# A gated cross-attention with a mixture of experts: shorter routing, another root, a folded bias

## What is computed

```python
x = x + tanh(g_xattn) * xattn(layernorm(x), ctx)    # 8 x 128 channels x 256, 16 heads of 8 channels
x = x + tanh(g_ffn) * ffn(layernorm(x))             # 1024 tokens of 256, 32 experts + a shared one

# xattn:  q = Wq x + bq; k = Wk c + bk; v = Wv c + bv; p = softmax(q k / sqrt(8)); Wo (p v) + bo
# ffn, routing of a token:
scores = sigmoid(x @ w_router)                      # 32 experts
sfc = scores + corr_bias
group_scores = top_k(sfc.reshape(T, 8, 4), 2).sum(-1)   # the two best of each group of four
keep the 4 best groups; among their experts the 6 best by sfc
routed = sum over the 6 of scores[e] * expert_e(x)
shared = silu(x @ sh_gate) * (x @ sh_up) @ sh_down
```

## Time and profile before

| what | us |
|---|---|
| median of 3 runs | 622.77 (622.03 to 625.15) |
| the profiled execution | 628.55 |
| its span | 626.7 |
| VectorE busy in the span | 432.9 (69%) |
| TensorE busy | 426.3 (68%) |
| ScalarE busy | 285.9 (46%) |
| GpSimd busy | 218.3 (35%) |

### The profile page before, as it was taken

One profiled execution on the slowest core, in us unless ns is written; L12 is line 12 of the kernel. 1 busy time (PEld: TensorE's weight loads), 2 busy tenths in 40 slices (PEclk: granted clock), 3 DMA queues, 4 the chain that ended last, 5 costly groups with the idle time before them and its releaser, 6 DMA issues.

```text
span 626.7 us, 12441 instructions
## 1 busy us (share of the span) xinstructions
PE 426.3 (68%) x3273; PEld 255.4 (41%) x3274; DVE 432.9 (69%) x1172; ACT 285.9 (46%) x505; POOL 218.3 (35%) x352
## 2 busy tenths in 40 slices
PE   0146677767766587566675754969999996999910
PEld 0113233233332243323232233747777774677700
DVE  8728559779898898888989488425655553555547
ACT  1056383936628355383444331326556552555500
POOL 8323001312322523225041417004555553555520
PEclk9998588988877977789788687979999999999965
DMA  7854544343362633625331257934677786874266
GB/s 217 279 132 157 205 150 149 95 132 125 91 220 75 211 98 111 227 74 211 121 122 51 80 166 224 343 107 149 202 256 256 251 276 228 253 253 137 81 257 245
DMA packets 70333, 109.96 MB, mean 175 GB/s; under 512 B 11863, under 2 KB 57015, under 8 KB 70295
## 3 DMA queue, kind: packets, MB, share of 16 engines
q1 hardware_dynamic: 50054, 75.32, 37.0%
q10 hardware_dynamic: 14144, 15.96, 8.6%
q0 software_dynamic: 6096, 18.23, 7.6%
HBM read 59.95 MB, written 49.53 MB: 175 GB/s over the span
## 4 chain that ended last, share of the span: by engine, by line
DVE 36%; PE 22%; issue 22%; DMA 10%; SPq 5%; ACT 4%; POOL 1%; DVEq 1%; ACTq 0%; POOLq 0%; PEldq 0%
DVE nmx L1153 7%; DMA wide<-split_weights 7%; PE ps L1038 4%; PE ps L1058 3%; DVE pk L1282 3%; PE ps L841 3%; DVE pk L1279 3%; PE ps L858 2%; DVE rD L1178 2%; PE ps L860 2%; PE ps L828 2%; SPq L426 2%; DVE q2S L1161 1%; PE ps L1050 1%; ACT wide L608 1%
## 5 line engine op out<-in xcount | busy, mean ns | idle before, releaser
L1038 PE MATMUL ps<-wide,bxT 128*128 x474 | 85.5, 317 | 8.2 <-ACT bxT L740 8.2
L1153 DVE TENSOR_REDUCE nmx<-ps 128x4 f32<-128x1024 f32 x64 | 76.6, 1220 | 16.4 <-PE ps L828 14.8
L1420 DVE SCALAR_TENSOR_TENSOR bh<-ps,bx,bsg 128x176 f32<-128x176 f32 x79 | 31.7, 401 | 79.9 <-ACT bsg L756 43.7
L614 ACT ACTIVATE wide<-ps 128x1024 f32<-128x1024 f32 x64 | 65.1, 1023 | 47.0 <-PE ps L841 46.7
L570 POOL DMA_INDIRECT picked_rows<-by,bid x79 | 78.2, 990 | 15.0 <-POOL tick L569 13.1
L740 ACT ACTIVATE bxT<-ps 128x512 f16<-128x512 f16 x79 | 47.2, 597 | 53.5 <-issue 21.2
L1058 PE MATMUL ps<-wide,bhT 88*128 x474 | 65.0, 273 | 0.6 <-DVE bhT L1428 0.4
L828 PE MATMUL ps<-wide,qS 128*128 128x512 f16 x128 | 43.4, 450 | 29.6 <-DVE nmx L1153 21.9
L841 PE MATMUL ps<-wide,kB 128*128 128x512 f16 x128 | 47.2, 456 | 14.3 <-ACT wide L614 8.5
L1038 PEld LDWEIGHTS ps<-wide,bxT 128*128 128x128 f16 x474 | 43.8, 99 | 25.7 <-issue 9.0
L530 POOL DMA_INDIRECT rows_by_expert<-pay,place x48 | 49.4, 1029 | 12.4 <-issue 11.4
(11 more groups left out here) (219 smaller groups left out, 847.5 us busy)
## 6 DMA issues: line engine op xcount, KB each, us to landing
split_weights<-pk SPq DMA_DIRECT2D x32, 608.0 KB
wide<-split_weights SPq DMA_DIRECT2D x32, 608.0 KB
bx<-rows_by_expert ACTq DMA_DIRECT2D x79, 160.0 KB
raw<-in_L_ffn_gate_w SPq DMA_DIRECT2D x32, 176.0 KB
raw<-in_L_ffn_up_w SPq DMA_DIRECT2D x32, 176.0 KB
raw<-in_L_ffn_down_w SPq DMA_DIRECT2D x32, 176.0 KB
rows_by_expert<-filling SPq DMA_DIRECT2D x1, 4960.0 KB, 15.5
rows_by_expert<-filling SPq DMA_DIRECT2D x20, 160.0 KB
```

The costliest lines, as they stand in the source:

```text
L614: act.activation(Pb[:, u % NP, :, :], ring(f"B{u}").rearrange("p (g t) -> p g t", g=NG), ACT.Exp, scale=SCALE).then_inc(emptied[slot(f"B{u ...
L1038: last = pe.matmul(ps[:, buf, 0:2 * M], bxT[:, buf, a, k, :], ring_w[:, bass.ds(given[u] + (2 * k + w) * 2 * M, 2 * M)], start=(n == 0), s ...
L1153: dve.tensor_reduce(nmx[:, tc, J, :, ROW], ring(f"A{u}").rearrange("p (g s) -> p g s", g=NG), AXX, ALU.max, negate=True).then_inc(emptied[ ...
```

## The change

Routing goes from 30 to 16 steps, in parts of 7, 4 and 5. The score becomes that of before divided by 64 (the factor of the weights, applied to the sum under the reciprocal), with a correction divided by 64 beforehand (corr_ws), so that the payload needs no factor. The sum of the two best of four is taken as the greatest of both pairs' sums and the sum of the pairs' maxima. For the selection, the values lie beside 4 (groups) or 2 (experts) columns that hold a huge value, so that MAX8 returns those and exactly 4 or 6 real values; MATCH_REPLACE marks the first place of each of the eight with another huge value. Chosen is what holds the mark. A copy that nobody reads stands ahead of MAX8 and MATCH_REPLACE.

The root's rounds have two operations, each with scalars read from a tile. The mean is not formed; x is multiplied by 256 and the sum subtracted. The bias of v is not added in norm_o: TensorE multiplies it once by Wo, and it is added to Wo's bias (bias_o). Behind the periods, the last batch's part 0 comes ahead of the places of the one before, parts 1 and 2 behind shared(3); GpSimd sends all six rows of that batch ahead of the low halves of the last tokens.

```diff
-ROUTE_STEPS = 30
+ROUTE_STEPS = (7, 4, 5)
+ROUTED = sum(ROUTE_STEPS)
@@ GpSimd, behind its periods
-            period(B + 1, B + 1)
+            fill_row(B + 1, (B + 1) % 2)
+            send(B - 2, (B - 2) % 2)
+            low_tokens(B + 1)
             send(B - 1, (B - 1) % 2)
@@ ScalarE, exp_logits
-                    act.wait_ge(rt_step, ROUTE_STEPS * (n - 3) + 5)
+                    act.wait_ge(rt_step, ROUTED * (n - 3) + 1)
@@ TensorE, setup
             project(ring("A1"), 0, 0, proj0_filled)
+            pe.matmul(od(1)[:, 0:1], wT[:, 3, :], bias[:, 2:3], start=True, stop=True).then_inc(bias_filled, 1)
@@ VectorE, setup
+            dve.memset(group[:, 0, GROUPS:], TOP)
+            dve.memset(masked[:, 0, NE:], TOP)
...
+            dve.wait_ge(consts_in, 16 * 12)
+            dve.tensor_scalar(corr_ws[:, :], corr[:, :], 1.0 / WS, None, ALU.mult)
+            dve.wait_ge(bias_filled, 1)
+            dve.tensor_scalar(bias_o[:, :], od(1)[:, 0:1], bias[:, 3:4], None, ALU.add)
@@ norm_o
-                step(dve.tensor_tensor(on[:, :], od(par)[:, 0:T], rD[:, :], ALU.mult))
-                step(dve.tensor_scalar(ob[:, :], on[:, :], bias[:, 2:3], None, ALU.add))
+                step(dve.tensor_tensor(ob[:, :], od(par)[:, 0:T], rD[:, :], ALU.mult))
@@ residual
-                step(dve.tensor_scalar(mv2[:, 0:1], st2[:, 0:1], 1.0 / T, None, ALU.mult))
-                step(dve.tensor_scalar(xc[:, :], xs[:, c, :], mv2[:, 0:1], None, ALU.subtract))
+                step(dve.tensor_scalar(xc[:, :], xs[:, c, :], float(T), st2[:, 0:1], ALU.mult, ALU.subtract))
@@ norm_x1
+                for i in range(3):
+                    root, better = s0[:, i % 2:i % 2 + 1], s0[:, 1 - i % 2:2 - i % 2]
+                    step(dve.tensor_scalar(s1[:, :], root, root, ve2[:, 0:1], ALU.mult, ALU.mult))
+                    step(dve.tensor_scalar(better, s1[:, :], -3.0 * scale * scale, root, ALU.add, ALU.mult))
@@ route
+                def choose(values, i):
+                    dve.tensor_copy(unread[:, :], values[:, 0, 0:8])
+                    step(dve.max(best8[:, i, :], values[:, 0, :]))
+                    dve.tensor_copy(unread[:, :], best8[:, i, :])
+                    step(dve.match_replace(values[:, 1, :], best8[:, i, :], values[:, 0, :], CHOSEN))
                 if part == 0:
+                    step(dve.tensor_scalar(rt[:, 0, :], el[:, :], 1.0, WS, ALU.add, ALU.mult))
+                    step(dve.reciprocal(score, rt[:, 0, :]))
+                    step(dve.tensor_tensor(choice, score, corr_ws[:, :], ALU.add))
...
+                    step(dve.tensor_tensor(high, pair[:, :, :, 0], pair[:, :, :, 1], ALU.max))
+                    step(dve.tensor_tensor(sums[:, :, 0:2], pair[:, :, :, 0], pair[:, :, :, 1], ALU.add))
+                    step(dve.tensor_tensor(sums[:, :, 2], high[:, :, 0], high[:, :, 1], ALU.add))
+                    step(dve.tensor_reduce(group[:, 0, 0:GROUPS], sums[:, :, :], AXX, ALU.max))
                 elif part == 1:
+                    choose(group, 0)
+                    step(dve.tensor_scalar(barred, group[:, 1, 0:GROUPS], CHOSEN, -3.0e38, ALU.is_lt, ALU.mult))
+                    step(dve.tensor_tensor(by_groups, choice.rearrange("p (g q) -> p g q", g=GROUPS),
+                                           barred.unsqueeze(2).to_broadcast([128, GROUPS, NE // GROUPS]), ALU.add))
                 else:
+                    choose(masked, 1)
+                    chosen = masked[:, 1, 0:NE]
+                    step(dve.tensor_scalar(em16[:, :], chosen, CHOSEN, None, ALU.is_equal))
                     dve.wait_ge(pay_step, 3 * c + 3)
+                    step(dve.scalar_tensor_tensor(out=pay[:, par, T:T + NE], in0=chosen, scalar=CHOSEN, in1=score,
+                                                  op0=ALU.is_equal, op1=ALU.mult))
+                    step(dve.tensor_tensor_scan(pay[:, par, T + NE:PAY], ones[:, 0:NE], em16[:, :],
+                                                slot_base[:, par:par + 1], ALU.mult, ALU.add))
@@ VectorE, behind the periods
+            wait_emptied(dve, "LG", B + 1)
+            route(0, B - 1, (B - 1) % 2)
             last_places(B - 2)
-            wait_emptied(dve, "LG", B + 1)
-            for part in range(3):
-                route(part, B - 1, (B - 1) % 2)
             shared(3)
+            route(1, B - 1, (B - 1) % 2)
+            route(2, B - 1, (B - 1) % 2)
             last_places(B - 1)
```

More of the change, by code:

```diff
@@ L24 @@
 ROW = 3 * KC
-ROUTE_STEPS = 30
+ROUTE_STEPS = (7, 4, 5)
+ROUTED = sum(ROUTE_STEPS)
 RSQRT_STEPS = 11
+ROOT_STEPS = 9
+O_STEPS = 2
+X1_STEPS = 4
+TOP, CHOSEN = 3.3e38, 3.2e38
 RSQRT_C = -2.0 ** 13
@@ L531, in send, with low_tokens @@
                                                  pay[:, par, :], None).then_inc(sent[par], 16)
+            def low_tokens(n):
+                wait_emptied(pool, "XT", n)
+                nc.gpsimd.tensor_tensor(xT[:, n - 2, :, 1, :], xT32[:, :, :], xT[:, n - 2, :, 0, :], ALU.subtract)\
+                    .then_inc(xT_lo, 1)
             def period(kind, n):
@@ L541, in period @@
                     elif job == "xT" and has(kind, "XT"):
-                        c = n - 2
-                        wait_emptied(pool, "XT", n)
-                        nc.gpsimd.tensor_tensor(xT[:, c, :, 1, :], xT32[:, :, :], xT[:, c, :, 0, :], ALU.subtract)\
-                            .then_inc(xT_lo, 1)
+                        low_tokens(n)
                     elif job == "values" and 1 <= kind < B:
@@ L1185, in residual @@
                 wait_filled(dve, "WO", n)
-                step = link(dve, x1_step, 5 * c, 5)
-                dve.tensor_scalar(wo_t[:, :], ring("WO")[:, 0:T], bias[:, 3:4], tg[:, 0:1], ALU.add, ALU.mult)\
+                step = link(dve, x1_step, X1_STEPS * c, X1_STEPS)
+                dve.tensor_scalar(wo_t[:, :], ring("WO")[:, 0:T], bias_o[:, 0:1], tg[:, 0:1], ALU.add, ALU.mult)\
                    .then_inc(emptied[slot("WO")], 1)
@@ new lines, in norm_x1 @@
+                step = link(dve, rs_step, ROOT_STEPS * c, ROOT_STEPS)
+                step(dve.tensor_scalar(s1[:, :].bitcast(I32), ve2[:, :].bitcast(I32), 1, None, ALU.logical_shift_right))
+                step(dve.tensor_scalar(s0[:, 0:1].bitcast(I32), s1[:, :].bitcast(I32), -1.0, 1597463007.0, ALU.mult,
+                                       ALU.add))
+                scale = 1.0
+                for i in range(3):
+                    root, better = s0[:, i % 2:i % 2 + 1], s0[:, 1 - i % 2:2 - i % 2]
+                    step(dve.tensor_scalar(s1[:, :], root, root, ve2[:, 0:1], ALU.mult, ALU.mult))
+                    step(dve.tensor_scalar(better, s1[:, :], -3.0 * scale * scale, root, ALU.add, ALU.mult))
+                    scale = -2.0 * scale * scale * scale
@@ new lines, in norm_x1 @@
+                assert scale == RSQRT_C
+                step(dve.tensor_scalar(xn2[:, :], xc[:, :], s0[:, 1:2], 1.0 / (RSQRT_C * T), ALU.mult, ALU.mult))
+            def route(part, c, par):
+                step = link(dve, rt_step, c * ROUTED + sum(ROUTE_STEPS[:part]), ROUTE_STEPS[part])
+                score, choice, barred = rt[:, 1, :], rt[:, 2, :], rt[:, 9, 0:GROUPS]
+                by_groups = masked[:, 0, 0:NE].rearrange("p (g q) -> p g q", g=GROUPS)
+                def choose(values, i):
[3 more added lines that the diff above has]
+                    step(dve.match_replace(values[:, 1, :], best8[:, i, :], values[:, 0, :], CHOSEN))
+                if part == 0:
+                    step(dve.tensor_scalar(rt[:, 0, :], el[:, :], 1.0, WS, ALU.add, ALU.mult))
+                    step(dve.reciprocal(score, rt[:, 0, :]))
+                    step(dve.tensor_tensor(choice, score, corr_ws[:, :], ALU.add))
+                    pair = choice.rearrange("p (g a b) -> p g a b", a=2, b=2)
+                    high = rt[:, 3, 0:16].rearrange("p (g a) -> p g a", a=2)
+                    step(dve.tensor_tensor(high, pair[:, :, :, 0], pair[:, :, :, 1], ALU.max))
+                    step(dve.tensor_tensor(sums[:, :, 0:2], pair[:, :, :, 0], pair[:, :, :, 1], ALU.add))
+                    step(dve.tensor_tensor(sums[:, :, 2], high[:, :, 0], high[:, :, 1], ALU.add))
+                    step(dve.tensor_reduce(group[:, 0, 0:GROUPS], sums[:, :, :], AXX, ALU.max))
+                elif part == 1:
+                    choose(group, 0)
+                    step(dve.tensor_scalar(barred, group[:, 1, 0:GROUPS], CHOSEN, -3.0e38, ALU.is_lt, ALU.mult))
+                    step(dve.tensor_tensor(by_groups, choice.rearrange("p (g q) -> p g q", g=GROUPS),
+                                           barred.unsqueeze(2).to_broadcast([128, GROUPS, NE // GROUPS]), ALU.add))
+                else:
+                    choose(masked, 1)
+                    chosen = masked[:, 1, 0:NE]
+                    step(dve.tensor_scalar(em16[:, :], chosen, CHOSEN, None, ALU.is_equal))
@@ L1257, in route @@
                     dve.wait_ge(pay_step, 3 * c + 3)
```

(7 more changed lines are left out.)

70 lines of the change are left out of this document (17 added, 53 removed).

## The result

The changed kernel took 594.83 us (median of 4 runs, 594.06 to 596.45), the kernel before on the same chip 623.86 (622.03 to 625.15): a ratio of 0.954, 95% interval 0.950 to 0.958. Its profiled execution took 595.5 us with a span of 593.4.

The account below looks back on a forecast made before the run. VectorE was taken to bound the kernel up to 330 us and again after 358.4. Gains of 14.8 + 3.7 + 3.5 + 0.3 + 6.1 = 28.4 us from the 622.77 us median gave 594.4 us, range 588 to 602 (eight in ten).

Parts of the forecast that it names:

- the main step: Up to 330 us, whatever VectorE no longer does comes off the time, if nothing else is as late.
- Rival D: Routing: MATCH_REPLACE far dearer than MAX8, from 2.1 us each cancelling the gain; 630 us at 2.5 us each; chance 0.02.
- C: Routing part 1: GpSimd collisions go as the copies slip through, part 1 takes 1.1 us, total 588 us; chance 0.16.
- Looped periods: Four looped attention periods: 3.7 us less each from routing, norm_o, residual and root, 14.8 us in all.
- rival A: Periods: second bound from ScalarE's masking and three shared banks, 599 to 603.5 us; sign: new VectorE waits over 1 us; chance 0.18.
- The fit "within 0.1 us": Looped period: VectorE, 3.5 us earlier, wants the transposed maxima at about 243.7 us, when they end, so it just fits.
- Period behind the loop: Period from 293.6 us: same gain as a looped period without collisions on either side, 3.7 us.
- Last attention period: Period from 330.3 us: TensorE's 4.5 us wait for the route ahead of the ranking matmul shortens; 3.5 us gained.
- Early part: Periods one and two, without route parts 1 and 2: 0.2 to 0.4 us less each, 0.3 counted; setup 0.
- Tail: From 358.4 us to the routed blocks: 0.7 + 3.2 + 3.4 - 1.1 = 6.2 us, taken as 6.1.
- let SyncE keep its pace: Tail: SyncE's eight expert loads still end at 388.5 us, its paddings land at 406.9, bounding only from 6.6 us gain.
- rival B: Tail: SyncE's loads slow, its last padding lands after ScalarE's; 3 us gain instead of 6.1, 597.5 us; chance 0.10.

Follow-up runs that it names:

- the control: The changed kernel, unedited, run again on the third chip: 596.4 us, ratio 0.9597 to the kernel before.
- guard_by_sum: Changed kernel with the two unread copies replaced by sums of the same eight columns: 596.59 us, ratio 0.9619 to the kernel before.
- order_back: Changed kernel with the old order behind the periods on VectorE and GpSimd: 594.13 us, ratio 0.9536 to the kernel before.
- cool_control: Changed kernel with 18 unread VectorE additions delaying the last attention period's routing, on the third chip: 600.84 us, ratio 0.9692 to the kernel before.
- before_again: The kernel before, unchanged, run again for a second trace: 618.88 us beside 622.13, ratio 0.9957.
- pads_early: Changed kernel with SyncE's 20 paddings behind its sixth expert load instead of its eighth, on the second chip: 609.09 us, ratio 0.9693 to the kernel before.
- pads_control: Changed kernel with SyncE's paddings behind the sixth expert load, repeated on the third chip: 594.38 us, ratio 0.9567 to the kernel before.
- warm_p8: Kernel before with 18 unread matmuls filling TensorE's wait in the last attention period, on the second chip: 628.65 us, ratio 0.9996.
- cool_warm_p8: Changed kernel with 18 unread VectorE additions and 18 unread matmuls in the last attention period, second chip: 611.02 us, ratio 0.9724 to the kernel before.

## Why the prediction was right, and where it was off

The time (594.83 for 594.4) was right, and so was the main step, that what VectorE no longer does in a period comes off the time. But the agreement is better than the terms, and part of it is luck: the last attention period gave 3.4 us more than its term, and the early part, the loop, the period behind it and the tail 4.0 us less than theirs.

**Prices of the small operations.** MATCH_REPLACE 0.36 us with its copy (0.38), the Newton pair 0.27 and 0.21 (0.27 and 0.21), part 2 1.5 us (1.42), part 1 without collisions 1.05 us in the period behind the loop (1.09), in the loop 2.07 (2.3). The prices from the nearest rows held. Rival D, a dear MATCH_REPLACE, is out, and so is C: the copies are held. One reading was wrong: the reciprocal takes 0.35 us of part 0's 1.2 (L1238), not most of them. That there are two entries is what the Trainium skill says (VectorE: DVE Perf Modes, section "Two Vector instructions with no wait between them"), and the trace agrees. But the load takes 0.08 us; to count it as another pass of 0.19, as I did for the comparison, was too much.

**Looped periods: 13.6 us for 14.8.** VectorE comes to q2S 4.6 us earlier in each period (the sum had 4.1), and then waits for TensorE, which it did not do there before: 3.7 us over the four periods in the first profile after, 4.1 in the control. That is rival A in small, and the sign that the prediction had named for it, new waits of over 1 us, is there in two of the four periods. The fit "within 0.1 us" was real at a granted clock of 1.00: there the wait is 0.2 to 0.3 us, and the period 35.2 to 35.5. Where the clock fell ahead of L940 the period is 36.5 to 36.9, and the prediction had no term for that. guard_by_sum shows that a further 0.7 us would have bought nothing. Behind q2S the four periods lost 0.9 us together, less than the 1.6 of the sum, though part 0 was mis-sized: in three of the four it takes 1.8 to 2.2 us instead of 1.6, with operations held to 0.30 and 0.34 us or a gap of 0.19 or 0.29 us.

**Period behind the loop: 3.2 for 3.7.** VectorE now waits 1.3 us for TensorE at L1194, ahead of kB, where it did not before: the clock at 0.50 behind q2S (above). At 1.00 (order_back, guard_by_sum) the gain is 4.4 us: the term was 0.7 us too small, and left out 1.2 us of the clock.

**Last attention period: 6.9 for 3.5.** The step failed twice: the sum left out norm_o (0.4 us), and mainly it took TensorE's work behind the wait as fixed. Cutting TensorE's wait from 3 to 4.5 us to 1.1 also gave back 1.4 us (cool_control), and 4.3 against the profile before, whose stretch was at the lower level nearly throughout. I had read the wait of 4.5 us without looking at the granted clock of what came behind.

**Early part: 0.3 gained by the prediction, 0.6 lost.** This isn't the change: between 45 and 55 us the granted clock was 0.91 in the profile before and 0.50 in the one after, but 0.50 in before_again as well. guard_by_sum, with the whole change and 0.89 there, comes to the first reciprocal at 99.14 us, the kernel before at 99.30.

**Tail: 4.7 for 6.1.** The counts came 6.4 us earlier, for 6.2, and ScalarE's last padding 5.8 to 7.4. Behind it the step failed that let SyncE keep its pace: in the first profile after, its eight loads took 31.65 us instead of 30.15 and its paddings landed last. That is rival B's mechanism and its sign, at 4.6 us of gain and not its 3. In the control the loads took 28.93 us and ScalarE's padding was last, yet the blocks' loads began 3.4 us behind its issue instead of 2.4 as in both profiles before: the gain was 4.8. So B is a bound in some executions, and in the others the landing takes most of the same amount.

**Whole time.** The blocks' stage behind the loads takes 208.3 to 215.8 us in the five profiles with the old routing (212.7 on the mean) and 208.7 to 213.3 in the nine with the new (210.2). Whether the old kernel loses some 2 us there stays open, and one pair of spans (33.3 us) says less than the mean over both pairs (27.2). The gain was 29.0 us in the first measurement and 24.4 with the control, with intervals that meet. On the second chip of the experiments the changed kernel itself did not run, but pads_early and pads_control are the same code: 19.5 us under the kernel before on the one chip and 26.4 on the other (0.9693 and 0.9567, intervals apart). In the profile of the slower one the four looped periods sum to 150.1 us instead of 144.1 and the last takes 24.0 instead of 19.8; warm_p8, with the old routing on that chip, has 158.8 us in the loop, as the old kernel has elsewhere. What stops the changed one there stays open.

## What to carry to other kernels

Price small VectorE operations by the nearest row of the same shape and count scalars read from a tile (0.05 to 0.06 us each): three operations replaced by two with more such scalars were worth nothing. After a large cut on the bounding engine, look at which wait has begun to grow, and shorten that engine by a little more as a test: if the wait takes it all, the next cut belongs elsewhere. Compare the two period by period, and at the same granted clock of TensorE, or the clock's swings hide the answer. When a change shortens an engine's wait, read TensorE's granted clock behind that wait, since the wait may have been paid twice; and where a new wait of TensorE has grown, read it there too.

## What the runs showed of the hardware that I had not expected

- A longer wait of TensorE (4.5 us instead of 1.1) took its granted clock in the next stretch from 1.00 to 0.80, and the same 78 matmuls from 6.6 to 8.1 us. Unread matmuls in the wait kept it at 1.00 (cool_warm_p8, warm_p8). Two executions of one kernel differed there by 2.9 us (10.9 at 0.57, 8.0 at 0.80).
- Behind waits of 1.4 us in the loop the granted clock sometimes fell and sometimes stayed, in one execution of one kernel, and the matmuls behind took 3.8 to 4.3 us or 2.7.
- MATCH_REPLACE8 costs little more than MAX8: from its start to the next step's it takes 0.25 to 0.28 us for 12 or 34 columns (0.08 for the load of the eight values, 0.15 to 0.18 for the replacement), MAX8 takes 0.19 to 0.22.
- A hold by GpSimd does not simply vanish with the operation that took it: of three, two went and one moved to the next tensor_scalar (0.17 to 0.52 us).
- Identical code gained 3.1% on one chip and 4.3% on another, each against the kernel before on the same chip.
